# One Silu pass for both heads of a pair, and an earlier place for the copy of the second half of the sums, in the first attention stage of a decoder kernel

## What is computed

```python
scores = jnp.einsum('bhtd,bhsd->bhts', q, k) * ATTNSCALE
key_self = jnp.clip(jnp.sum(k * k, axis=-1), 1e-06, None)
w = jax.nn.softplus(scores / jnp.sqrt(key_self)[:, :, None, :])
w = jnp.where(causal, w, 0.0)
w = w * jax.nn.sigmoid(SCALE * w)
w = jnp.where(w < sinks, 0.0, w)
total = jnp.sum(w, axis=-1, keepdims=True) + sinks + 1e-06
out = jnp.einsum('bhts,bhsd->bhtd', w / total, v) + (sinks / total) * v_null
y = jnp.einsum('bntc,ncd->bntd', context, W_O) + W_O_bias[None, :, None, :]
return y.mean(axis=1)
```

## Time and profile before

| what | value |
|---|---|
| median of 3 runs | 2972.34 us (2963.99 to 2972.50) |
| the profiled execution | 2978.33 us, of which its span is 2976.5 us |
| PE busy in the span | 2667.9 us (90%) |
| DVE, ACT, POOL busy | 1781.1 (60%), 1560.2 (52%), 801.8 us (27%) |
| Silu passes (line 510) | 128 of 1536 columns, mean 1473 ns |
| Softplus passes (line 491) | 192 of 1024 columns, mean 1024 ns |
| thresholds (line 685) | 512 of 384 columns, mean 734 ns |

### The profile page before, as it was taken

One profiled execution on the slowest core, in us unless ns is written; L12 is line 12 of the kernel. 1 busy time (PEld: TensorE's weight loads), 2 busy tenths in 40 slices (PEclk: granted clock), 3 DMA queues, 4 the chain that ended last, 5 costly groups with the idle time before them and its releaser, 6 DMA issues. The chain is left out here.

```text
span 2976.5 us, 49262 instructions
## 1 busy us (share of the span) xinstructions
PE 2667.9 (90%) x18536; PEld 2086.4 (70%) x18536; DVE 1781.1 (60%) x4040; ACT 1560.2 (52%) x3054; POOL 801.8 (27%) x889
## 2 busy tenths in 40 slices
PE   5999999999866899999979999999969999859998
PEld 4556656565455567677669888989957777648887
DVE  3567665675447556665456666767765656454444
ACT  2777666776534344444445565656546656542221
POOL 1133222232111344444521111111006656600000
PEclk8799998998678899999989999999989999979999
DMA  3000000000012111111010000000020000020000
GB/s 114 5 4 5 5 1 4 5 5 1 1 47 75 32 45 27 26 26 28 22 43 4 6 6 6 3 1 1 1 73 5 8 5 5 1 100 8 8 8 29
DMA packets 88763, 59.42 MB, mean 20 GB/s; under 512 B 55120, under 2 KB 78416, under 8 KB 88016
## 3 DMA queue, kind: packets, MB, share of 16 engines
q1 hardware_dynamic: 88528, 56.25, 6.4%
HBM read 39.46 MB, written 8.39 MB: 16 GB/s over the span
## 5 line engine op out<-in xcount | busy, mean ns | idle before, releaser
L685 DVE SCALAR_TENSOR_TENSOR a_w<-a_w,a_sinks 128x384 f32<-128x384 f32 x512 | 348.5, 734 | 124.3 <-ACT a_w L510 123.9
L2034 POOL TENSOR_SCALAR x_weights<-x_weights,x_sums 128x256 f32<-128x256 f32 x256 | 232.5, 928 | 271.8 <-DVE x_sums L2093 271.8
L1124 POOL TENSOR_SCALAR f_weights<-f_weights,f_sums 128x256 f32<-128x256 f32 x256 | 232.7, 928 | 267.9 <-DVE f_sums L1354 267.9
L338 PE MATMUL psum<-a_qT,a_kT_half 32*128 32x512 f32 x768 | 244.0, 720 | 21.7 <-ACT a_w L491 19.6
L491 ACT ACTIVATE a_w<-psum 128x1024 f32<-128x1024 f32 x192 | 188.1, 1024 | 132.5 <-PE psum L343 132.1
L343 PE MATMUL psum<-a_future,a_unit 32*128 32x128 f32 (+5 forms) x1536 | 238.7, 436 | 0.0
L1282 ACT ACTIVATE f_weights<-psum,f_negmax 128x256 f32<-128x256 f32 x256 | 117.9, 473 | 210.1 <-DVE f_negmax L1348 210.1
L343 PEld LDWEIGHTS psum<-a_future,a_unit 32*128 32x128 f32 x1536 | 136.6, 215 | 111.1 <-issue 110.2
L1619 ACT ACTIVATE a_turned_w_hi<-psum 128x512 fp32r<-128x512 f32 x256 | 139.1, 596 | 142.5 <-PE psum L1529 142.4
L2004 ACT ACTIVATE x_weights<-x_masked_s,x_negmax 128x256 f32<-128x256 f32 x256 | 127.0, 497 | 137.1 <-DVE x_negmax L2085 137.1
L1736 DVE TENSOR_REDUCE a_negmax<-psum 128x1 f32<-128x1024 f32 x128 | 156.6, 1224 | 55.7 <-PE psum L119 51.4
(11 more groups left out here) (357 smaller groups left out, 7402.1 us busy)
## 6 DMA issues: line engine op xcount, KB each, us to landing
f_xnT<-all_xnT_all SPq DMA_DIRECT2D x16, 256.0 KB, 2.4
f_pv_rows<-f_pv SPq DMA_DIRECT2D x8, 512.0 KB, 3.2
f_pv_groups<-f_pv_rows SPq DMA_DIRECT2D x8, 512.0 KB
f_w<-in_f_w SPq DMA_DIRECT2D x2, 2048.0 KB, 10.3
all_x_all<-in_x SPq DMA_DIRECT2D x1, 2048.0 KB, 8.5
a_xnT<-all_xnT_all SPq DMA_DIRECT2D x8, 256.0 KB, 2.3
x_xnT<-all_xnT_all SPq DMA_DIRECT2D x8, 256.0 KB, 2.3
x_ctxT<-in_x_ctxT SPq DMA_DIRECT2D x8, 256.0 KB, 3.0
```

Of the source, the lines that this page charges most:

```text
L338: pe.matmul(psum[:, 2 * x + h, :], kT_half[rows[h], step % 2, g, keys], queries, start=True, stop=False)
L685: ins = dve.scalar_tensor_tensor(part, part, sinks[:, col:col + 1], part, ALU.is_ge, ALU.mult)
L1124: ins = pool.tensor_scalar(w, w, sums[:, k, h, t:t + 1], None, ALU.mult)
L2034: ins = pool.tensor_scalar(w, w, sums[:, k, h, t:t + 1], None, ALU.mult)
```

## The change

ScalarE runs Silu over both heads of a pair in one pass of 3072 columns, where it ran two of 1536. So a quad has two passes in place of four. The copy of the second half of the sums stands behind the first of the two passes; before, it stood behind the third of the four. A threshold waits for the pass of its pair, where it waited for that of its head. No instruction of another engine changes; VectorE's threshold waits for another count of the same semaphore.

```diff
@@ -505,11 +505,10 @@
                                 k, n = quad
                                 act.wait_ge(plus_done, (n * 2 + 2) * SLOTS)
                                 for pair in range(2):
-                                    for h in range(2):
-                                        wu = w[:, (2 * n + pair) % PAIR_RING, h].rearrange("p r t -> p (r t)")
-                                        act.activation(wu, wu, ACT.Silu, scale=SILU_SCALE).then_inc(silu_done, 1)
-                                        if (pair, h) == (1, 0):
-                                            take_sums(sums_quad, 1, spare_bank(b, step, "sum", 1))
+                                    wu = w[:, (2 * n + pair) % PAIR_RING].rearrange("p h r t -> p (h r t)")
+                                    act.activation(wu, wu, ACT.Silu, scale=SILU_SCALE).then_inc(silu_done, 1)
+                                    if pair == 0:
+                                        take_sums(sums_quad, 1, spare_bank(b, step, "sum", 1))
                             if ahead and step == 4:
 
                                 act.preload_act_table_set("natural_log_exp_and_others")
@@ -678,7 +677,7 @@
 
                 k, n = quad
                 pair, h = head // 2, head % 2
-                dve.wait_ge(silu_done, n * 4 + head + 1)
+                dve.wait_ge(silu_done, n * 2 + pair + 1)
                 for r in (2 * half, 2 * half + 1):
                     part = w[:, (2 * n + pair) % PAIR_RING, h, r, :]
                     col = r * NH + 4 * k + pair + 2 * h
```

## The result

The changed kernel takes 2991.09 us in the median (2982.27 to 2995.43); before, it was 2972.42 (2963.99 to 2975.31, four executions each). The ratio is 1.0064, 95% interval 1.0033 to 1.0094. The prediction was 2973.5 us in a range of 2960 to 2989: the time lies above the range. So the first comparison shows a loss, the second one just doesn't tell it from none; its size is better read from the stage.

A forecast was written before the change was run, and what follows sets the result against it. TensorE, busy 90% of the span, was taken to wait for ScalarE in this stage. Waits +0.3, step 6's clock -8.5 and step 4's +9.6 made +1.4 us on the median 2972.34, given as 2973.5; range 2960 to 2989.

The forecast's parts named there:

- The pass: ScalarE's Silu of 3072 columns: takes 2.80 us, between 2.75 and 2.85.
- Step 4's wait: TensorE's wait for a Softplus in step 4: grows by 0.98 us to 2.57, 6 times, +5.9 us.
- Step 6: TensorE's wait before out: 1.90 to about 0.45 us, 5 times, -7.1; clock stays up, -8.5 us.
- Step 0: Wait before step 0's first q projection shrinks, VectorE's rotation waited for next: -0.2 us, 6 times, -1.2 us.
- The ends of the stage: Last step's threshold chain starts later, +1.3 us; first and last batch, +1.4; together +2.7 us.
- The clock of step 4: Half-clock stretch behind step 4's longer wait grows: 1.6 us a batch, 6 times, +9.6 us.
- Rival 1: Step 4's low clock holds until step 6: +4.8 us a batch, over 0.3% slower from two of six; chance 0.26.

The follow-up runs named there:

- the second one: The changed kernel measured again against the kernel before, on the chip of the last experiments: 2984.98 us, ratio 1.0022 (0.9997 to 1.0047).
- e5: Kernel before, with Ln and Exp of the next batch's keys' norm moved from step 4 to step 6, behind its first slot's Softplus: 2925.10 us, ratio 0.9823.
- e6: Changed kernel, with Ln and Exp of the next batch's keys' norm moved from step 4 to step 6: 2904.46 us, ratio 0.9763 to the kernel before.
- e2_merge_but_step4: The change in steps 0, 2 and 6 only, step 4 keeping four passes and the old copy place, against the kernel before: 2956.48 us, ratio 0.9936.

## Why the prediction was wrong, step by step

- **The pass.** Taken as 2.80 us between 2.75 and 2.85; measured 2.760. Right. The 0.83 ns a column of the lower bound stood in no row; the wide pass gives (2.760 - 1.473) / 1536 = 0.838. By the Trainium skill (ScalarE: Activation LUTs, "What ACT_TABLE_LOAD costs") a pass with immediate scale and bias takes 186 ns and 0.833 ns a column, which makes an estimate of 2.745 us; the trace agrees with its 2.760.
- **Step 4's wait.** Forecast 2.57, measured 2.54. Right, and for the reason given.
- **Step 6.** Forecast a wait of 0.45 (its own sum gives 1.90 - 1.42 = 0.48) and a clock that stays up; measured 0.44 and 1.00. The mechanism is right, but it was counted five times and came twice: where the low clock runs into step 6, TensorE arrives late by itself. Of the 7.1 + 8.5 us forecast, 7.8 came in the six batches.
- **Step 0.** Forecast -0.2 us, with VectorE's rotation as the next wait. That wait came, with 0.48 us before the fourth projection (TensorE's timeline, step 0 of batch 3), and the step went from 21.86 to 21.79 us. Over the six batches it is 0.9 us, of 1.2 forecast. Right.

```profile
348.66 1.13 PE L386 MATMUL psum<-all_xnT_all,a_wq 128*128 128x256 f32 x4 [0.48 <-DVE a_rot L633]
```

- **The ends of the stage.** Forecast +2.7 us; what lies behind batch 7's step 2 grew by 0.4 us (840.9 - 728.21 = 112.7 against 852.5 - 739.42 = 113.1) and what lies between the first Silu and batch 1's step 2 by 0.3 (169.42 - 78.50 = 90.92 against 171.12 - 79.88 = 91.24), so this term was too large by some 2.
- **The clock of step 4: the step that failed.** I priced its growth at 1.6 us a batch, from the one batch with a stretch of 13.7 us, and called that the nearer of two ends. The batches went to the other end: four of six at 23.9 us or more. The sum also took it that step 4's clock leaves step 6 alone. Steps 4 and 5 grew by 18.2 us in the six batches, where the terms +5.9 and +9.6 made 15.5; the larger miss is the 7.8 us of step 6's gain that the long stretches ate. Rival 1 had this case, with the point from which it decides (two of six) and a price of 4.8 us a batch; measured are 55.2 - 51.1 = 4.1. It had a chance of 0.26, because one batch in six of the one trace looked like a rare coincidence. The other two traces with the old wait have it in 5 of 12 batches, so the one trace was a favourable draw, and I read a frequency from it.
- By the terms of the sum the six steady batches were to become 1.3 us shorter (5.9 + 9.6 - 7.1 - 8.5 - 1.2); they became 9.5 longer. The last step of the sum has a slip of 0.2: 2972.34 + 1.4 is 2973.7 and not 2973.5.

In step 4, 1.6 to 2.6 us of idleness were followed by half clock in 41 of the 42 batches of the table; without them (e5, e6) the clock stayed up in 10 of 12, and fell for 3.4 us in the others. The rule that the prediction named from the Trainium skill (TensorE: Matmul & The Clock Gate, "A second HAM failure mode: psum-queue depth-cycling"), by which small idle times between groups of matmuls make the clock swing, agrees with that.

**What stays open.** Why the low stretch ends after 10 to 14 us in one batch and after 24 in the next. The work is the same, and no run here shows what decides it or sets it on purpose; the counts above suggest that a longer wait makes the long ones more frequent, but 6 of 18 against 14 of 24 isn't proof. What a long stretch costs is shown, and that without the wait no stretch of 10 us or more begins in steps 4 and 5 of the six batches. Nor is it shown why the clock still fell for 3.4 us in step 5 in two batches of e5. Nor was it tried whether step 0's wait for VectorE can be had back.

## What to carry to other kernels

A copy that moves to an earlier place in an in-order engine takes its wait along, and everything behind it waits too. So look in each kind of step at whether the producer is done by the new place; here it was in one of four, and late by half a microsecond in two and by one in the step where somebody stood waiting at the end of the chain. Price an idle time of TensorE with the low clock behind it, not by its own length: 1.6 us of waiting cost 6 us a batch here (29.10 in step 4 of the kernel before, 23.11 without the wait), and the cure was to move two small instructions and their table load out of the chain, after which the same change was worth 20 us (2925.10 to 2904.46). And a stretch whose length differs between equal batches of one trace has a distribution; take its frequency from several traces, and carry both ends in the range, with what lies behind the stretch.

## What the runs showed of the hardware that was not expected

- With the same instructions behind the same wait of 1.6 us the clock stayed at half for 10.2, 13.7, 23.9 or 27.3 us in batches of one execution (e2_merge_but_step4).
- 0.93 us of idleness in step 0 (338.82 in the earlier trace rows) was followed by no fall of the clock, 1.59 us in step 4 nearly always; in one batch of e2_merge_but_step4 it wasn't, and in two of the six of e5_ln_step6 the 1.90 us before out wasn't.
- Behind a wide Silu the next instruction starts 2.67 us after its own start (319.26 to 321.93), behind two of 1536 columns 2 x 1.376 = 2.752. The merge itself saves 0.08 us a pass, almost nothing, where passes already follow one another.
